# One-core gated-recurrence and mixture-of-experts layer: wider up-projection products, the token tile in a PSUM bank of its own, nested end tests, expert rows stored by lower and higher expert

## What is computed

```python
# attn: a gated recurrence in log space
k = xn @ W_z.T + b_z
log_coeffs, log_z = -softplus(k), -softplus(-k)
log_values = [log h0, log_z + g_log(xn @ W_h.T + b_h)]
a_star = pad(cumsum(log_coeffs, axis=-1))
log_h = a_star + cumlogsumexp(log_values - a_star, axis=1)
log_h = (log_h - mean) / std            # over everything
x = exp(log_h)[:, 1:] + xn;  attn = layernorm(x) * ln_w + ln_b
# ffn: 8 experts, the best 2 of each token
w, sel = top_k(softmax(xn @ w_gate.T), 2);  w = w / sum(w)
for e in range(8):
    h = silu(xn @ w1[e].T) * (xn @ w3[e].T)       # 704 wide
    out += h @ w2[e].T * (weight of e for the token)
```

## Time and profile before

| what | value |
|---|---|
| median of three runs | 462.13 us |
| profiled execution, its own time | 460.31 us |
| its span | 458.6 us |
| granted clock of PE, mean | 0.907 of full |
| PE, DVE, ACT, POOL busy | 353.7, 263.2, 222.3, 199.9 us |
| PE waits for DVE before `x_tile` (L1224) | 48.4 us in 28 tiles |

### The profile page before, as it was taken

The page is one execution under the profiler, slowest core; times in us unless marked ns, Lnnn a source line. Parts: engine busy times, 40 slices in busy tenths (PEclk is TensorE's granted clock), DMA queues, the critical chain, the costliest instruction groups (busy, mean ns, idle before and its releaser), DMA issues.

```text
span 458.6 us, 7159 instructions
## 1 busy us (share of the span) xinstructions
PE 353.7 (77%) x2056; PEld 312.0 (68%) x2056; DVE 263.2 (57%) x464; ACT 222.3 (48%) x331; POOL 199.9 (44%) x212
## 2 busy tenths in 40 slices
PE   0699998897878898687988879899987677888300
PEld 0694543697667787586887878799986667887300
DVE  5307899466555647645588543454577564733047
ACT  2434957442867854478662259835624341223000
POOL 6250075027636544845676465527734563222000
PEclk9999979798998999889999989999999797889565
DMA  8750022004224221322142364214320010001069
GB/s 293 275 177 0 1 71 89 2 13 121 74 66 121 73 80 34 110 84 68 38 154 93 70 194 160 79 26 129 92 76 25 11 36 24 24 25 26 16 232 328
DMA packets 21873, 41.46 MB, mean 90 GB/s; under 512 B 2337, under 2 KB 15137, under 8 KB 21825
## 3 DMA queue, kind: packets, MB, share of 16 engines
q1 hardware_dynamic: 14784, 26.74, 18.4%
q0 software_dynamic: 3728, 10.10, 7.1%
q10 hardware_dynamic: 3312, 3.94, 2.6%
HBM read 31.60 MB, written 9.18 MB: 89 GB/s over the span
## 4 chain that ended last, share of the span: by engine, by line
PE 46%; DVE 25%; ACT 10%; issue 9%; DMA 5%; ACTq 2%; POOL 1%; POOLq 0%; DVEq 0%; SPq 0%
PE PS L1269 20%; PE PS L1254 7%; PE PS L1281 5%; ACT hT L569 4%; PE PS L1156 3%; DVE xn L1022 3%; DVE tmp L926 3%; PE PS L1224 3%; DVE xn L1134 3%; PE PS L1185 3%; ACT wbuf L583 3%; DMA small_sb<-small 3%; ACT L690 2%; DVE hT L921 2%; PE PS L1197 2%
## 5 line engine op out<-in xcount | busy, mean ns | idle before, releaser
L1254 PE MATMUL PS<-wbuf,xT 128*128 128x384 f32 (+1 forms) x864 | 149.9, 330 | 1.2 <-issue 1.2
L1254 PEld LDWEIGHTS PS<-wbuf,xT 128*128 128x128 f32 x864 | 140.9, 190 | 2.5 <-issue 2.5
L1269 PE MATMUL PS<-wbuf,hT 128*128 128x256 f32 x648 | 102.5, 320 | 11.5 <-issue 10.8
L1269 PEld LDWEIGHTS PS<-wbuf,hT 128*128 128x128 f32 x648 | 93.7, 221 | 19.5 <-issue 19.2
L410 POOL TENSOR_TENSOR wbuf<-raw,wbuf x28 | 76.6, 2745 | 34.9 <-ACT wbuf L583 34.2
L921 DVE TENSOR_TENSOR hT<-PS,hT 128x768 fp32r<-128x768 f32 x36 | 34.5, 958 | 93.0 <-ACT hT L569 91.4
L391 POOL DMA_INDIRECT work<-xn_dram,gcol x39 | 41.8, 1072 | 30.2 <-POOL gcol L389 27.1
L1224 PE MATMUL PS<-ident,work 128*128 128x128 f32 x74 | 16.5, 306 | 49.4 <-DVE tmp L926 48.4
L574 ACT ACTIVATE tmp<-PS 128x384 f32<-128x384 f32 x72 | 32.1, 457 | 40.8 <-PE PS L1254 35.6
L598 ACT ACTIVATE work<-PS 128x256 f32<-128x256 f32 x36 | 13.7, 381 | 75.8 <-PE PS L1269 75.8
L926 DVE TENSOR_TENSOR tmp<-tmp,PS 128x384 f32<-128x384 f32 x72 | 35.0, 515 | 26.7 <-ACT tmp L574 26.3
(11 more groups left out here) (183 smaller groups left out, 417.7 us busy)
## 6 DMA issues: line engine op xcount, KB each, us to landing
raw<-w_main SPq DMA_DIRECT2D x24, 544.0 KB
raw<-w_main SPq DMA_DIRECT2D x8, 416.0 KB
xn_dram<-xn SPq DMA_DIRECT2D x4, 512.0 KB, 3.3
U<-x ACTq DMA_DIRECT2D x2, 1024.0 KB
...
```

Of the source, the lines that this page charges most:

```text
L1254: ins = pe.matmul(dst, xT[:, slot, xpart, q * P:(q + 1) * P], wbuf[:, w, wpart, base + a:base + b], start=(q == 0 and xpart == 0 and wpart ...
L1269: ins = pe.matmul(y_ps, hT[:, hpart, c * P:(c + 1) * P], wbuf[:, w, wpart, W13 + c * D:W13 + (c + 1) * D], start=(c == 0 and hpart == 0 an ...
```

## The change

Five things are changed, and a few steps in the middle change places.

1. `up` has 18 products instead of 24. The host lays w1 and w3 side by side for the column ranges 0 to 255, 256 to 511 and 512 to 703, so one product makes both: 512, 512 and 384 columns wide. The two parts that `silu` and `gate` work on are now 512 and 192 columns.
2. `xT_ps` has bank 5 for itself and PE's wait for `gate(j)` before `x_tile(j+1)` is gone. `hT_ps` moves to banks 3 and 4.
3. The small inputs come in two loads: the gate weights, biases and `h0` (22 columns) ahead of ACT's four input loads, the rest behind them. PE waits for the second load only before `project`. POOL normalises three tiles of four, ACT one, and `normal(g)` comes earlier on ACT.
4. The tests at the end are nested: the test for j + 1 stands inside the body for j, and the last steps follow once for all cases.
5. `hot1` and `hot2` stand for the lower and the higher expert of a token instead of the best and the second, so the first half of `y_dram` holds the lower expert's rows. The weights are reordered to match (eight small DVE instructions). The last tile is one of the highest expert, so its rows are all in the second half. POOL reports all other rows first (`s_rows` 1) and the last tile's later (`s_rows` 2). SP loads `U` after the first report and `A` after the second.

In the middle, `cumsum(0)` comes one projection earlier, `cumsum(1)` comes before `project(3, 1)`, and DVE's `softplus(0)`, `softplus(1)` come before `tile_experts` and `add_cumsum(0)` right after it.

```diff
-SPLIT = 3 * P
-HALVES = [(0, SPLIT), (SPLIT, F)]
+PARTS = [(0, 256), (256, 512), (512, F)]
+SPLIT = 512
...
-        w1_ps = [PS[:, 2 * n * 512:2 * n * 512 + b - a] for n, (a, b) in enumerate(HALVES)]
-        w3_ps = [PS[:, (2 * n + 1) * 512:(2 * n + 1) * 512 + b - a] for n, (a, b) in enumerate(HALVES)]
-        hT_ps = PS[:, 4 * 512:4 * 512 + HC * P]
-        xT_ps = PS[:, 0:2 * 512].rearrange("p (q n) -> p q n", q=Q)[:, :, SPLIT:SPLIT + P]
+        up_wide = PS[:, 0:2 * 512].rearrange("p (n m c) -> p n m c", n=2, m=2)
+        w1_ps = [up_wide[:, :, 0, :], PS[:, 2 * 512:2 * 512 + F - SPLIT]]
+        w3_ps = [up_wide[:, :, 1, :], PS[:, 2 * 512 + F - SPLIT:2 * 512 + 2 * (F - SPLIT)]]
+        hT_ps = PS[:, 3 * 512:3 * 512 + HC * P]
+        xT_ps = PS[:, 5 * 512:5 * 512 + D].rearrange("p (q n) -> p q n", q=Q)
...
             used = eng.value_load(tiles[0:1, 0:1], min_val=SURE, max_val=NTILES)
-            for j in range(SURE, NTILES):
+
+            def nest(j):
                 with eng.If(used > j):
                     tile((j - 1) // LOOP, (j - 1) % LOOP)
+                    if j + 1 < NTILES:
+                        nest(j + 1)
+                    if drain:
+                        drain(j)
                     eng.nop(nofuse=True)
+            nest(SURE)
             if end:
-                for j in range(SURE, NTILES + 1):
-                    with eng.If(used == j):
-                        end(j)
-                        eng.nop(nofuse=True)
+                end(used)
...
             sp.wait_ge(s_p2, 4 * NT // 2)
-            sp.wait_ge(s_rows, 1)
             for k, buf in ((0, U), (1, A)):
+                sp.wait_ge(s_rows, k + 1)
...
             for g in range(4):
                 pool.wait_ge(s_mr, g + 1)
-                for t in range(4 * g, 4 * g + 4, 2):
+                for t in (4 * g, 4 * g + 2, 4 * g + 3):
...
             def end(used):
-                scatter(used - 1, (used - 1) % DEEP)
                 for k in range(DEEP):
-
-                    pool.wait_ge(s_gt[k], 16 * len(range(k, min(used + DEEP, NTILES), DEEP)))
-                    pool.wait_ge(s_st[k], 16 * len(range(k, used, DEEP)) + 16)
+                    pool.wait_ge(s_gt[k], 16 * len(range(k, SURE + DEEP, DEEP)))
+                    pool.wait_ge(s_st[k], 16 * len(range(k, SURE - 1, DEEP)) + 16)
                 pool.sem_inc(s_rows, 1)
-            tail(pool, tile, end)
+                pool.wait_ge(s_y, used + 1)
+                pool.tensor_copy(scol[:, DEEP:DEEP + 1], sidx[:, ds(used - 1, 1)]).then_inc(s_sc, 1)
+                hold(pool, s_sc, used)
+                pool.indirect_dma_start(y_dram, bass.IndirectOffsetOnAxis(scol[:, DEEP:DEEP + 1], 0),
+                                        hst[:, 0:D], None).then_inc(s_end, 16)
+                pool.wait_ge(s_end, 16)
+                pool.sem_inc(s_rows, 1)
+            tail(pool, tile, end, drain)
...
+            act.dma_start(small_sb[:, 0:FIRST], small[:, 0:FIRST]).then_inc(s_small, 16)
             for g in range(1, 8, 2):
...
-            act.dma_start(small_sb[:, :], small).then_inc(s_small, 16)
+            act.dma_start(small_sb[:, FIRST:], small[:, FIRST:]).then_inc(s_large, 16)
...
+            ia, ib = idx8[:, 0:NT], idx8[:, NT:2 * NT]
+            dve.tensor_tensor(near[:, 0:NT], ia, ib, ALU.min)
+            step(dve.tensor_tensor(near[:, NT:2 * NT], ia, ib, ALU.max))
+            dve.scalar_tensor_tensor(te(hot1), ramp, float(P), over_e(near[:, 0:NT]), ALU.subtract, ALU.is_equal)
...
-                    for n, (a, b) in enumerate(HALVES):
-                        if n and late:
+                    for parts in ((0, 1), (2,)):
+                        if late and 2 in parts:
                             late()
                         for q in range(Q):
                             for xpart, wpart in ((0, 0), (0, 1), (1, 0)):
-                                for dst, base in ((w1_ps[n], q * 2 * F), (w3_ps[n], q * 2 * F + F)):
-                                    ins = pe.matmul(dst, xT[:, slot, xpart, q * P:(q + 1) * P],
-                                                    wbuf[:, w, wpart, base + a:base + b],
+                                for n in parts:
+                                    at, cols = 512 * n, 2 * (PARTS[n][1] - PARTS[n][0])
+                                    ins = pe.matmul(PS[:, at:at + cols], xT[:, slot, xpart, q * P:(q + 1) * P],
+                                                    wbuf[:, w, wpart, q * 2 * F + at:q * 2 * F + at + cols],
...
                 if not isinstance(j, int) or j < NTILES - 1:
-                    pe.wait_ge(s_g, 2 * j + 1)
                     x_tile(j + 1, (2 + u) % DEEP, 16 * i + 16 * ((2 + u) // DEEP + 1))
```

More of the change, by code:

```diff
@@ L476, in normal @@
                 act.wait_ge(s_mr, g + 1)
-                for t in range(4 * g + 1, 4 * g + 4, 2):
-                    act.activation(xn[:, t, :], xn[:, t, :], ACT.Identity, scale=rstd[:, t:t + 1],
-                                   bias=nmean[:, t:t + 1]).then_inc(s_xo, 1)
+                t = 4 * g + 1
+                act.activation(xn[:, t, :], xn[:, t, :], ACT.Identity, scale=rstd[:, t:t + 1],
+                               bias=nmean[:, t:t + 1]).then_inc(s_xo, 1)
             def evacuate(m):
@@ L520, in _ @@
             deviations(0)
+            normal(0)
             deviations(1)
[L522 removed]
+            normal(1)
             evacuate(0)
             deviations(2)
[L525 removed]
+            normal(2)
             evacuate(1)
[L527 removed]
             deviations(3)
[L529 to L530 removed]
             normal(3)
[L532 removed]
+            for m in range(2, 8):
                 evacuate(m)
@@ L571, in silu @@
             def silu(j):
-                for n, (a, b) in enumerate(HALVES):
+                for n in range(2):
                     act.wait_ge(s_up, 2 * j + (n + 1))
-                    act.activation(sl[:, a:b], w1_ps[n], ACT.Silu).then_inc(s_silu, 1)
+                    act.activation(sls[n], w1_ps[n], ACT.Silu).then_inc(s_silu, 1)
             def split_due(before, j):
@@ L704, in _, with last_copy @@
                         done = tile(i, u, done, None, x_again if j == 18 else None)
-            tail(act, tile, lambda used: y_copy(used - 1, (used - 1) % DEEP, 16 * ((used - 1) // DEEP) + 16))
+            def last_copy(used):
+                act.wait_ge(s_dn, used)
+                act.activation(hst[:, 0:D], y_ps, ACT.Copy).then_inc(s_y, 1)
+            tail(act, tile, last_copy)
         @block.vector
@@ L1038, in _ @@
             step(dve.tensor_tensor(w12[:, 1, :], w12[:, 1, :], w12[:, 0, :], ALU.mult))
+            for k in range(2):
+                for v in range(2):
+                    ins = dve.tensor_tensor(w_of[:, 2 * k + v, :], w12[:, v, :], first_low[:, (k + v) % 2, :], ALU.mult)
+            step(ins)
+            for k in range(2):
+                ins = dve.tensor_tensor(w12[:, k, :], w_of[:, 2 * k, :], w_of[:, 2 * k + 1, :], ALU.add)
+            step(ins)
             dve.wait_ge(s_u0b, 2)
```

75 lines of the change are left out of this document (43 added, 32 removed).

## The result

| | before | after |
|---|---|---|
| median of the runs, us | 460.14 (455.53 to 462.76, 4 runs) | 392.53 (390.43 to 393.23, 4 runs) |
| ratio, 95% interval | | 0.855 [0.846, 0.864] |
| span of the profiled execution, us | 458.6 | 391.1 |
| start of `up(1)` | 89.75 | 85.43 |
| 34 intervals, `up(1)` to `up(35)` | 325.1 (9.56 each) | 270.7 (7.96 each) |

The forecast was 403 in a range of 388 to 430. The span lost 67.5 us: 54.4 in the loop, 8.8 at the end, 4.3 ahead of `up(1)`.

What follows compares the result with a forecast made beforehand. PE's 48.4 us of waits for DVE's `gate` before `x_tile`, with `down` queued behind, were taken to bound the loop. Loop 39, start 5.5, middle 0 and end 12 made 56.5 us off 460.31: 403 us, range 388 to 430.

Steps and rivals of the forecast that it cites:

- waits in the loop, less what comes back: Tile loop: 40 us of PE waits removed, less 3 us of returning branches and waits and 3 us of POOL delaying DVE.
- PE's own work in the loop: low clock, products: Tile loop: 3 us from fewer slow `down` steps and 2 us from fewer `up` products.
- start: Before the last logits: PE begins at about 8.6 instead of 15.13 us; 5.5 us won, bounds 3 and 6.5.
- middle: Around the last projection: earlier `cumsum(1)` frees `up(0)`, but ACT's chain starts later; 0 us, bounds 2 either way.
- end: After the last tile: nested tests start `down(35)` 5.6 us earlier and `U` loads before the last scatter; 12 us, bounds 7 and 14.
- The mechanism: Tile loop: the wait before `x_tile` goes, `x_tile` and `down` run while ACT and DVE work; next wait is before `h_tile`.
- The cap of 2.2 us: Tile loop: at most 2.2 us won per removed wait; five longer waits exceed it by 8.1 us, leaving 40.3 of 48.4.
- `down` at the low clock: Tile loop: about nine `down` behind long waits run 1.3 to 1.8 us longer; between 0 and 12 us won, 3 taken.
- the second rival: Tile loop: the clock stays high, slow `down` give 12 us instead of 3, returned costs are 2 instead of 6; 390, chance 0.12.
- 18 products for 24: `up` in each tile: six fewer products save 0.11 us per tile, 4 us in 36 tiles, half of it counted: 2 us.
- The first rival: Tile loop: DVE delayed beside POOL's weight pieces makes PE wait again; loop gives 20 us instead of 39; 423, chance 0.25.
- the ring: Tile loop: PE, ACT and DVE wait for each other around `x_tile` and `gate`, with `down` caught in it; 48.4 us of waits.

Runs made afterwards that it cites:

- after_third: The kernel after, unchanged, run once more beside later experiments: 394.34 us, ratio 0.859.
- e3_narrow: The kernel after with 36 products in `up` instead of 18, 256 and 192 columns wide, over the same columns: 396.58 us, ratio 0.867.
- e7_short: The kernel after with POOL's 28 weight pieces in the loop cut to an eighth of their columns, part of the computation left out: 371.52 us, ratio 0.809.
- e8_before_short: The kernel before with POOL's 28 loop weight pieces cut to an eighth of their columns, part of the computation left out: 442.43 us, ratio 0.961.
- e1_wait_x: The kernel after with PE's wait for the first part of `gate(j)` put back before `x_tile(j+1)`: 465.68 us, ratio 1.018.
- e5_rows_one: The kernel after with the load of `U` held until the last scatter has landed, as before: 395.50 us, ratio 0.864.
- e10_old_end: The kernel after with the old tests one after another and the load of `U` held until the last scatter has landed: 398.98 us, ratio 0.867.
- e9_raw_late: The kernel after with SP's weight loads held until x arrived, and ACT's first logits copies before its second normalisations: 391.05 us, ratio 0.852.
- e6_tests_flat: The kernel after with the old tests at the end, one behind another instead of nested: 394.01 us, ratio 0.859.
- after_again: The kernel after, unchanged, run again beside the first experiments: 394.56 us, ratio 0.862.

## Why the prediction was right, and which terms were not

The terms, against the two profiled executions:

| term | forecast | measured |
|---|---|---|
| waits in the loop, less what comes back | 40 - 3 - 3 = 34 | PE's idle time -35.8 |
| PE's own work in the loop: low clock, products | 3 + 2 = 5 | PE's busy time -18.6 |
| start | 5.5 | 3.5 |
| middle | 0 | 0.8 |
| end | 12 | 8.8 |
| sum | 56.5 | 67.5 |

**The mechanism was right.** PE no longer waits at `x_tile`, `down` runs under `gate`, and the wait that is left lies before `h_tile`: 13.1 us, forecast 10 to 15, though in 8 tiles and not 15. The cap of 2.2 us on each removed wait, and 6 us that come back, gave 34 for 35.8, or for some 41 with the 5.7 us of overlap that the view counts as busy time. A pause that the sum did not have goes with the waits: `down` followed `x_tile` by 0.5 to 0.8 us where PE had waited, and follows by 0.14 now. The experiments with the wait put back confirm the mechanism, with one correction: nearly all of the gain needs `down` to be free, and freeing `x_tile` alone gives 5 us.

**The term that was mis-sized** is `down` at the low clock: "Between 0 and 12 us; I take 3". Nine slow `down` cost 13.7 us over 2.38 each before, and none is slow after. The reason I gave against it, that the next `up` would be slow instead, holds for three tiles and 4.7 us, so 9 us are left. With `x_tile` and the `cumsum` products, 4.4 us shorter, that gives the 13 us of the groups, for a forecast of 5. This is what the second rival described ("the clock stays high", 390, chance 0.12), and the result lies nearer to it than to the forecast. The Trainium skill, "TensorE: Matmul & The Clock Gate", section "Part 1: The HAM clock gate", makes activity the thing that releases the clock, so denser tiles gain twice; the granted clock of the loop, 0.93 to 0.97, agrees. I had cited this rule and given it too little weight. That the result fell within the range is in part because the range took this rival in.

The prediction also read the cause of the low clock too simply: "each time after PE stood for more than 5 us". That holds for the rows it names (5.66 and 8.18 us). The other eight slow `down` of the loop stand behind waits of 1.34 to 4.20 us, and others behind 2.09 and 1.75 us were fast (176.79 and 260.80). The length of the last pause alone does not decide. The kernel after shows it once more: `up(4)` stands behind the same pause of 2.4 to 2.6 us for a weight piece in eight traces with this `up`, and takes 4.1 us in five and 5.6 to 5.7 in three, as here in `after_third`:

```profile
112.78 5.65 PE L1297 MATMUL PS<-wbuf,xT 128*128 128x512 f32 x18 [2.46 <-POOL wbuf L422]
```

**18 products for 24** was counted with 2 us and won 0.02 us at most in a tile that PE bounds (3.93 for 3.93 to 3.95). The step that failed is the reading of 0.48 us over the ideal as a cost per product; in `e3_narrow` 24 products of 256 columns take as long as 12 of 512.

**The first rival** (DVE and POOL close the ring, 423) did not come. Its price existed, 22 us by `e7_short`, but it was there before as well, 17 us by `e8_before_short`. Only the difference, 5 us, is the change's doing, and I had counted 3.

**The start** came to 3.5 of 5.5. The forecast had PE's start right (8.6; it was 8.55) and noted that ACT's input loads are issued one load later, but costed this at nothing. They land 1.6 to 2.7 us later (two traces more of the kernel after have 7.1 and 8.2 us). It had the copies between normalisations at 1 us, and PE's two waits for them are 1.22 and 0.89.

**The end** came to 8.8 of 12. `down(35)` started 5.8 us earlier after `h_lo(35)`, for 5.6. The flat tests put back 3.6 to 4.3 of it, and `e1_wait_x` shows that nested tests alone don't ensure it. `down(35)` itself was 1.15 us shorter, for 0 to 1.8. The step that failed is the early load: it runs beside the last scatter, which took 4.8 us instead of the counted 2.4. `U` was also issued later than counted, 4.7 us after the scatter of tile 34 (364.04 to 368.75) instead of 3.7. But in `after_third` it came after 3.15 us (362.76 to 365.91), the scatter took 6.4, and the end was no shorter. `y_copy` to the end shrank by 1.8 us only; with the load held back in `e5_rows_one` it is 2.9 us longer.

The 11 us between the two sums are then: +13.6 from PE's work, +1.8 from the waits, -2 at the start, -3.2 at the end, and +0.8 in the middle. They partly cancel: 16 us too little against 5 too much.

## What to carry to other kernels

When a wait sits before a short step, look at what is queued behind it on the same engine: here the wait of two transposes of 0.4 us also held a `down` of 2.4 us that needed nothing, and that decided 60 us. Price a removed wait twice, once as idle time with a cap and once as the work that ran at the low clock behind it, by counting the slow instances in the trace and taking off the steps that become slow instead. And read a change at the end of a kernel in the trace and not in medians: a part that gives 4 us can look like nothing while another part hides it, and an early bulk load can slow the small transfer that everything waits for.

## What the runs showed of the chip

- A product with its weight load takes 173 ns at 384 columns, 147 at 320 and 110 at 192, at the high clock (from the starts of `silu`'s second part: 1.04, 1.77 and 1.32 us for 6, 12 and 12 products). The Trainium skill, "TensorE: Matmul & The Clock Gate", section "Wait — 56ns, not 53.3ns?", has N / 2.4 GHz and 2.5 ns from start to start, an estimate of 162, 136 and 82. The measured ones are 7 to 8% above it for the wide ones and a third for the narrow one; here the measurement decides.
- One addition of DVE over 512 columns takes 0.69 us alone and 2.85 beside two POOL pieces. With these cut to an eighth it took 0.85, and DVE's busy time in the loop fell by 21.7 us of a 391 us kernel. The Trainium skill, "SBUF — State Buffer", section "SBUF: two separate sides", calls the shared ports an exclusive lock for the whole instruction; the experiment agrees, in that a shorter POOL instruction shortens DVE's.
- A scatter of one tile took 2.6 to 2.8 us to the load that waits for it when it ran alone (before, `e5_rows_one`, `e8_before_short`, `e10_old_end`). With the 2 MB load issued 1.4 to 3.7 us ahead it took 4.6 to 6.9 us (eight traces, among them after and `e9_raw_late`: 367.65 to 374.09), with the load 5.7 us ahead 3.9 (`e1_wait_x`), and 6.5 us ahead 3.1 (`e6_tests_flat`). The Trainium skill, "DMA: Bandwidth & Descriptors", section "Queues, rings and completion order", says that each DMA engine takes turns between its queues packet by packet. These runs don't show the turns, only the price.
- With seven tests one behind another `down(35)` starts 4.3 to 6.3 us after `h_lo(35)` (four traces). The Trainium skill, "Advanced Engine Details and Errata", section "Control Flow Timing", has 108 ns for a compare-and-branch and 51 ns for a plain one, by estimate 1.1 us for seven of each. The section "Instruction fetch mechanics" of its page "Runtime: NRT & Kernel Launch" says that a taken branch out of the fetched window has to fetch first. That would fit the rest, and the 4.1 us of `e1_wait_x` with nested tests, but no run here separates it.
- A weight piece that comes late can stop PE too: `up(4)` waited 2.47 us for POOL at 113.43, a wait that the kernel before had not. In `after_third`, `e5_rows_one` and `e6_tests_flat` that `up` then ran at the low clock, and the interval of tile 4 was 10.1 us; in the kernel after, `after_again`, `e9_raw_late` and `e10_old_end` it was 8.6.
